# Two graph-attention layers on one core: layer 2's score rows made between the layers and kept in SBUF, its rows normalised on VectorE

## The chip, the cores and the metric

The kernel runs on 1 core of one Trainium2 chip. The metric is the device time of one execution in microseconds (us). Before the change it is 506.02 us, the median of 3 runs (504.74 to 507.35).

## What is computed

Two graph-attention layers over 4096 nodes with 64 features each. Each has a residual sum and a layer norm behind it. Cut to what matters:

```python
def _L0_gnn_ref(h, adj, a):                     # layer 1
    e = (h @ a[:D, 0])[:, None] + (h @ a[D:, 0])[None, :]
    e = jnp.where(e > 0, e, 0.01 * e)
    e = jnp.where(adj > 0, e, NEG_INF)
    return jax.nn.softmax(e, axis=1) @ h

def _L1_gnn_ref(x, edge_index, weight_w, weight_a, bias):   # layer 2
    wh = x @ weight_w
    e = (wh @ weight_a[:OUT_C, 0])[:, None] + (wh @ weight_a[OUT_C:, 0])[None, :]
    e = jax.nn.leaky_relu(e, negative_slope=0.01)
    scores = jnp.where(edge_index > 0, e, NEG_INF)
    return jax.nn.softmax(scores, axis=1) @ wh + bias

x = _layernorm(x + _L0_gnn_ref(x, adj, L0_gnn_a), axis=-1)
x = _layernorm(x + _L1_gnn_ref(x, adj, L1_gnn_weight_w, L1_gnn_weight_a, L1_gnn_bias), axis=-1)
```

`adj` is 4096x4096 int32 of zeros and ones, some four ones in a row.

## The kernel before, in words

The exponent of `leaky_relu(s_i + d_j)` is one of two products, `exp(s_i) exp(d_j)` or its power 0.01, by the sign of `s_i + d_j`. So the kernel never makes the 4096x4096 table of exponentials. It makes, in fp8 bytes that hold 0 or 1, a mask of the positive pairs and one of the negative pairs, and multiplies each with a table of the features, scaled by column and split into three bf16 parts.

The 4096 rows are cut into eight blocks of 512 (`NS`), the columns of a block into four granules of 1024 (`NG`, index `g`). For each granule:

- ScalarE makes the signs (`signs`, eight instructions of 128x512, L557): the input is the block's score row, the sum's row part for 512 rows spread over all 128 partitions, the bias is the column part `dcol`. A score row is one matmul of TensorE (`score_row`, L320) into one of two PSUM halves `srow`.
- VectorE ands the signs with the adjacency bytes (`mask`, L820, L823; granules 0 and 1 lie in SBUF in `kept`, granules 2 and 3 are reloaded by SyncE into `turned`).
- TensorE multiplies (`granule`, L418): 64 matmuls of 195 columns into four banks of the PSUM tensor `acc`.

`neg` and `pos` are rings of four granules; ScalarE may start a granule when TensorE is through with the one four before (semaphore `products`). After a block, VectorE reads `acc` (`read_acc`, L829), forms average, residual and moments (`average`, `residual_sum`, `moments`, L847 to L870), GpSimd takes the power -0.5 of the variance (L968) and multiplies the negated mean with it (L972), and ScalarE normalises the four row groups (`normalize`, L570). In layer 1 the result goes to `xn`; in layer 2 to `x1s`, from which SyncE stores.

Each engine runs its own stream, written out by hand. Between the layers TensorE's stream is, in this order: the last granule of layer 1; the turn of block 6's rows (`turn_x1`, L431); the score row of block 1; small products with the source vector (`scores1`, L371); the projection of block 6 (`project`, L401); more `scores1`; turn and projection of block 7; the first part of the column mean (`mean1`, L351); turn and spreading of the column maximum (L334, L338); the rest of `mean1`; the first granule of layer 2. ScalarE copies turned rows and projections (L577, L579, L585) in between, and makes the exponentials (L535, L536). In the loop of layer 2 each pass of TensorE is

```python
            with pe.Fori(1, NS - 2) as s:
                granule(1, s, NG - 1)
                score_row(1, s + 2)
                for g in range(NG - 1):
                    granule(1, s + 1, g)
```

`xy_old` holds layer 1's tables; layer 2's lie in `stage`. The program's functions that the change touches follow.

Of the kernel before, what the change touches and what calls it, by code (L numbers as in the profile page):

```python
# [36 lines left out]
BYTES = 4  # L37
# [5 lines left out]
def gat_kernel(nc, x, adj, a0, w1, a1, bias1, ident, out):  # L43
# [33 lines left out]
    with ctx:  # L77
# [63 lines left out]

        acc = ctx.enter_context(nc.psum_tensor("acc", [P, RB, 512], F32))
# [35 lines left out]
        srow_ready = sem("srow_ready")  # L178
        narrowed = sem("narrowed")
# [116 lines left out]
        def _(pe):  # L296
# [22 lines left out]
            def score_row(layer, s):  # L319
                nc.tensor.matmul(srow[:, bass.ds((s % 2) * 512, 512)], arep[:, layer, :], xT_at(s),  # L320
                                 start=True, stop=True).then_inc(srow_ready, 1)

# [151 lines left out]
            scores1(NS // 2, NS - 2)  # L474
            turn_x1(NS - 1)
# [4 lines left out]
            spread_max(1)  # L480
            mean1(2, NS - 2)

# [19 lines left out]
        def _(act):  # L502
# [40 lines left out]
            def signs(layer, s, g, tiles=range(GT)):  # L543
                k = (layer * NS + s) * NG + g
                if g == 0:
# [8 lines left out]
                o = neg[:, g, :].bitcast(I8).rearrange("p (b i e) -> p b e i", b=GB, e=BYTES)  # L554
                for t in tiles:
                    col = g * GT + t
                    last = nc.scalar.activation(o[:, t // BYTES, t % BYTES, :], srow[:, bass.ds((s % 2) * 512, 512)],  # L557
                                                ACT.Sign, bias=dcol[:, layer, col:col + 1])
# [3 lines left out]
            def normalize(layer, s):  # L562
                k = layer * NS + s
                act.wait_ge(std_ready, 2 * k + 2)
                if layer == 1:
                    act.wait_ge(stored, 16 * (s + 1))
                act.sem_inc(act_turn, 1)
                for r in range(RB):
                    to = x1s[:, r, :] if layer else xn[:, row_at(s, r), :].rearrange("p o d -> p (o d)")
                    last = nc.scalar.activation(to, y[:, r, :], ACT.Identity, bias=shift_n[:, r:r + 1],  # L570
                                                scale=rstd[:, r:r + 1])
# [443 lines left out]
```

## Time and profile before

| what | value |
|---|---|
| median of 3 runs | 506.02 us |
| profiled execution, its own time | 507.45 us |
| its span, first to last instruction | 505.7 us |
| busy share TensorE / VectorE / ScalarE / GpSimd | 88% / 80% / 79% / 18% |
| mean granted clock of TensorE over the span | 0.926 of full speed |
| HBM read, written | 77.74 MB, 9.44 MB |

The span is that of one execution of the program taken by the hardware profiler. Layer 1 lasts until some 285 us of it and streams the adjacency from HBM; layer 2 works on bytes that are on the chip or reloaded. A row of a view names the engine, the line of the program, what is written and read, and times in us. PE is TensorE, ACT is ScalarE, DVE is VectorE, POOL is GpSimd. PEclk is the granted clock of TensorE as a share of 2.4 GHz. A float32 matmul shows as two records. The share of a whole span is an average over stages with different limits, so the text goes by stretches.

### The profile page before, as it was taken

Reading aid. Unit: us, or ns where it says so; the run is one execution under the profiler, and the core shown is the slowest. Engines: PE = TensorE matmul, PEld = TensorE weight load, DVE = VectorE, ACT = ScalarE, POOL = GpSimd, SP = SyncE. Lnnn points to the kernel's source line nnn. Section 1 sums busy time; section 2 is a strip of 40 time slices with the busy share of each in tenths; the row PEclk is TensorE's granted clock in tenths of the full one; section 3 lists DMA queues with packets and bytes.
Section 4 is the critical chain, followed back from the end, with each engine's and each line's share of the span. In section 5 each row is a group of like instructions: output and inputs, shape, how many; then the busy total and the mean of one; then the engine's idle time right before and its main releaser. Section 6 shows DMA issues by size and latency. Waiting matters only on the chain.

```text
span 505.7 us, 11789 instructions
## 1 busy us (share of the span) xinstructions
PE 447.5 (88%) x4420; PEld 417.1 (82%) x4420; DVE 402.2 (80%) x712; ACT 397.8 (79%) x619; POOL 90.4 (18%) x68
## 2 busy tenths in 40 slices
PE   0799778879979899897979979999999999999991
PEld 0379768868979698797969968999999999999991
DVE  3789989889799898989887889794849586675844
ACT  2695269877978879887890938899899999999931
POOL 0012221514225151421423020010101010101010
PEclk9987979997979999897997958999999999999997
DMA  8999999999999999999973100202030202102000
GB/s 186 251 237 277 286 262 291 313 303 312 313 312 329 302 324 315 319 306 318 329 207 126 43 0 3 84 2 96 1 93 0 93 10 83 55 38 93 3 12 10
DMA packets 80294, 87.71 MB, mean 173 GB/s; under 512 B 7298, under 2 KB 76162, under 8 KB 80258
## 3 DMA queue, kind: packets, MB, share of 16 engines
q1 hardware_dynamic: 45602, 52.98, 36.9%
q10 hardware_dynamic: 34656, 34.21, 25.0%
q8 instruction: 27, 0.44, 0.4%
q14 instruction: 9, 0.07, 0.0%
HBM read 77.74 MB, written 9.44 MB: 172 GB/s over the span
## 4 chain that ended last, share of the span: by engine, by line
issue 49%; DVE 22%; DMA 18%; PE 5%; POOL 4%; SPq 1%; ACT 0%; POOLq 0%; ACTq 0%; DVEq 0%
DMA stage<-in_adj 16%; DVE narrow L791 4%; PE acc L418 4%; DVE turned L803 3%; POOL small L968 3%; DVE pos L817 2%; DMA xn<-in_x 2%; DVE num L854 1%; DVE num L861 1%; DVE red L847 1%; DVE kept L728 1%; DVE bn L866 1%; DVE num L851 1%; DVE kept L725 1%; DVE neg L820 1%
## 5 line engine op out<-in xcount | busy, mean ns | idle before, releaser
L557 ACT ACTIVATE neg<-srow,dcol 128x512 int8 (+1 forms) x512 | 352.9, 880 | 10.4 <-issue 8.0
L418 PE MATMUL acc<-xy_old,pos 128*128 128x195 bf16 x1024 | 198.9, 263 | 22.8 <-POOL pos L979 20.0
L418 PE MATMUL acc<-xy_old,neg 128*128 128x195 bf16 x1024 | 198.6, 263 | 0.0
L418 PE MATMUL acc<-stage,pos 128*128 128x195 bf16 x1024 | 178.2, 248 | 0.0
L418 PE MATMUL acc<-stage,neg 128*128 128x195 bf16 x1024 | 178.1, 248 | 0.0
L418 PEld LDWEIGHTS acc<-xy_old,pos 128*128 128x128 fp8e4 x1024 | 107.5, 105 | 31.7 <-issue 29.8
L418 PEld LDWEIGHTS acc<-xy_old,neg 128*128 128x128 fp8e4 x1024 | 106.8, 104 | 1.6
L418 PEld LDWEIGHTS acc<-stage,pos 128*128 128x128 fp8e4 x1024 | 100.8, 98 | 4.7 <-issue 4.5
L418 PEld LDWEIGHTS acc<-stage,neg 128*128 128x128 fp8e4 x1024 | 100.3, 98 | 0.3 <-issue 0.3
L791 DVE TENSOR_SCALAR narrow<-stage 128x4096 uint8<-128x4096 int32 x32 | 74.1, 2316 | 16.3 <-DMA stage<-in_adj 15.4
L968 POOL TENSOR_TENSOR small<-small,minus_half 128x4 f32<-128x4 f32 x16 | 36.6, 2288 | 210.7 <-DVE small L869 210.7
L820 DVE TENSOR_TENSOR neg<-neg,kept 128x1024 uint32<-128x1024 uint32 x32 | 39.1, 1223 | 31.5 <-ACT neg L557 30.9
L829 DVE TENSOR_REDUCE red<-acc 128x130 f32<-128x390 f32 x64 | 33.1, 553 | 21.3 <-PE acc L418 21.2
L979 POOL TENSOR_TENSOR pos<-kept,neg 128x512 uint32<-128x512 uint32 x16 | 22.3, 1392 | 142.5 <-DVE neg L820 142.5
L820 DVE TENSOR_TENSOR neg<-neg,turned 128x1024 uint32<-128x1024 uint32 x32 | 39.2, 1224 | 2.2 <-ACT neg L557 1.7
L979 POOL TENSOR_TENSOR pos<-turned,neg 128x512 uint32<-128x512 uint32 x16 | 22.3, 1393 | 54.6 <-DVE neg L820 53.8
L570 ACT ACTIVATE x1s<-num,small 128x64 f32<-128x64 f32 x32 | 11.5, 429 | 20.9 <-POOL small L972 20.7
L570 ACT ACTIVATE xn<-num,small 128x64 f32 (+1 forms) x32 | 11.5, 429 | 18.9 <-POOL small L972 18.9
L315 PE MATMUL acc<-idf,xn 128*64 128x128 f32 x32 | 7.2, 418 | 15.8 <-DMA xn<-in_x 15.8
L315 PEld LDWEIGHTS acc<-idf,xn 128*64 128x64 f32 x32 | 5.2, 170 | 18.4 <-issue 12.2
L823 DVE TENSOR_TENSOR pos<-turned,neg 128x1024 uint32<-128x1024 uint32 x16 | 19.6, 1224 | 0.6
L823 DVE TENSOR_TENSOR pos<-kept,neg 128x1024 uint32<-128x1024 uint32 x16 | 19.6, 1224 | 0.5
(117 smaller groups left out, 337.2 us busy)
## 6 DMA issues: line engine op xcount, KB each, us to landing
stage<-in_adj ACTq DMA_DIRECT2D x64, 512.0 KB, 9.2
stage<-in_adj SPq DMA_DIRECT2D x64, 512.0 KB, 9.4
spill<-turned SPq DMA_DIRECT2D x16, 512.0 KB, 7.5
turned<-spill SPq DMA_DIRECT2D x16, 512.0 KB, 3.8
out<-x1s SPq DMA_DIRECT2D x8, 128.0 KB, 1.9
xn<-in_x SPq DMA_DIRECT2D x1, 768.0 KB, 17.0
kept<-in_x SPq DMA_DIRECT2D x4, 128.0 KB, 3.9
kept<-in_x ACTq DMA_DIRECT2D x4, 128.0 KB, 5.0
```

The costliest lines, as they stand in the source:

```text
L315: last = nc.tensor.transpose(acc[0:D, t % RB, b * P:(b + 1) * P], xn[:, t // 2 * (2 * RB) + t % 2 + 2 * b, :], idf[:, :])
L418: last = nc.tensor.matmul(acc[:, r, c * XW:(c + 1) * XW], masks[c][:, t // BYTES, t % BYTES, r * P:(r + 1) * P], xy[layer][:, g * GT + t, ...
L557: last = nc.scalar.activation(o[:, t // BYTES, t % BYTES, :], srow[:, bass.ds((s % 2) * 512, 512)], ACT.Sign, bias=dcol[:, layer, col:col ...
L570: last = nc.scalar.activation(to, y[:, r, :], ACT.Identity, bias=shift_n[:, r:r + 1], scale=rstd[:, r:r + 1])
L791: nc.vector.tensor_scalar(narrow[:, 0:GN].rearrange("p (b g j) -> p g b j", b=GB, g=GR), stage[:, g % SLOTS, :].rearrange("p (g b j) -> p ...
L803: nc.vector.transpose(words(mask_at(s, g)), words(narrow[:, 0:GN])).then_inc(turned_ready, 1)
L817: nc.vector.scalar_tensor_tensor(words(pos[:, g, :])[:, half], c[:, half], CODES, a[:, half], ALU.bitwise_xor, ALU.bitwise_and).then_inc(p ...
L820: nc.vector.tensor_tensor(c, c, a, ALU.bitwise_and).then_inc(neg_ready, 1)
L823: nc.vector.tensor_tensor(words(pos[:, g, :]), a, c, ALU.bitwise_xor).then_inc(pos_ready, 1)
L829: nc.vector.tensor_reduce(red[:, r, :, :].rearrange("p c f -> p (c f)").rearrange("p (c f) -> p c f", c=2), acc[:, r, 0:2 * XW].rearrange( ...
L968: nc.gpsimd.tensor_tensor(rstd, var, minus_half[:, :], ALU.pow).then_inc(std_ready, 1)
L979: nc.gpsimd.tensor_tensor(pos[:, g, :].bitcast(U32)[:, half], mask_at(s, g).bitcast(U32)[:, half], neg[:, g, :].bitcast(U32)[:, half], ALU ...
```

## The change

It has two parts.

The score rows of blocks 2 to 7 of layer 2 are no longer made in layer 2's loop. TensorE makes rows 2 to 5 ahead of the turn of block 7, into the four banks of `acc`, and rows 6 and 7 behind the spreading of the column maximum (`score_rows`). ScalarE copies them in two instructions (`keep_rows`) into `rows_sb`, which lies over `xy_old`; layer 2's signs read them there from block 2 on. Blocks 0 and 1 read `srow` as before.

Layer 2's normalising leaves ScalarE. VectorE does it in four instructions (`normalize1`) behind the mask of the next block's granule 2, with the mean and GpSimd's power; GpSimd's second product and VectorE's negated mean fall away in layer 2.

```diff
+        rows_sb = xy_old[:, :].bitcast(F32)[:, 0:(NS - 2) * SUP].rearrange("p (s n) -> p s n", n=SUP)
...
+            def score_rows(first, end):
+
+                for s in range(first, end):
+                    last = nc.tensor.matmul(acc[:, (s - 2) % RB, :], arep[:, 1, :], xT_at(s), start=True, stop=True)
+                last.then_inc(rows_psum, 1)
...
             scores1(NS // 2, NS - 2)
+            pe.wait_ge(acc_read, NS * RB + RB)
+            score_rows(2, NS - 2)
             turn_x1(NS - 1)
...
             spread_max(1)
+            pe.wait_ge(rows_kept, 1)
+            score_rows(NS - 2, NS)
             mean1(2, NS - 2)
+            pe.wait_ge(rows_kept, 2)
 
             granule(1, 0, 0)
...
-            score_row(1, 2)
-            for g in range(NG - 1):
-                granule(1, 1, g)
-            with pe.Fori(1, NS - 2) as s:
-                granule(1, s, NG - 1)
-                score_row(1, s + 2)
-                for g in range(NG - 1):
-                    granule(1, s + 1, g)
-            granule(1, NS - 2, NG - 1)
-            for g in range(NG):
-                granule(1, NS - 1, g)
+            with pe.Fori(1, NS) as s:
+                for g in range(NG):
+                    granule(1, s, g)
...
+            def keep_rows(first, end):
+                n = end - first
+                act.wait_ge(rows_psum, 1 if first == 2 else 2)
+                act.wait_ge(products, FREE_AT_FIRST + NS * NG * RB)
+                nc.scalar.copy(rows_sb[:, first - 2:end - 2, :], acc[:, 0:n, :]).then_inc(rows_kept, 1)
...
             copy_wh(NS - 2)
-            normalize(0, NS - 1)
+            keep_rows(2, NS - 2)
+            normalize(NS - 1)
             copy_x1(NS - 1)
             copy_wh(NS - 1)
             act.wait_ge(shift_ready, 4)
             exps(1, slice(NEAR, TILES), minus_shift[:, 1, 0:1], minus_shift[:, 1, 1:2], far_exp)
+            keep_rows(NS - 2, NS)
             for g in range(2, NG):
                 signs(1, 0, g)
             signs(1, 1, 0)
             row_factors(1)
-            with act.Fori(0, NS - 2) as s:
-                for g in range(1, NG):
-                    signs(1, s + 1, g)
-                normalize(1, s)
-                signs(1, s + 2, 0)
             for g in range(1, NG):
-                signs(1, NS - 1, g)
-            normalize(1, NS - 2)
-            normalize(1, NS - 1)
+                signs(1, 1, g)
+            act.wait_ge(rows_kept, 2)
+            with act.Fori(2, NS) as s:
+                for g in range(NG):
+                    signs(1, s, g)
...
+            def normalize1(s):
+
+                dve.wait_ge(stored, 16 * (s + 1))
+                dve.wait_ge(std_ready, 2 * NS + s + 1)
+                dve.sem_inc(dve_turn, 1)
+                for r in blocks:
+                    last = V.tensor_scalar(x1s[:, r, :], y[:, r, :], mv[:, r, 0:1], rstd[:, r:r + 1],
+                                           ALU.subtract, ALU.mult)
+                last.then_inc(x1_ready, 1)
```

TensorE between the layers, from the second group of small products to the first granule of layer 2. Before:

```order
L371 MATMUL misc<-v_src,xT 128x1 x8
L431 MATMUL flip<-idf,xn 64x128 x4
L401 MATMUL misc<-wext,xTs 128x65 x4
L351 MATMUL flip<-wh,onesN 128x256 x2
L334 MATMUL misc<-idf,mcol 1x128
L338 MATMUL misc<-mcol,one_row 128x1
L351 MATMUL flip<-wh,onesN 128x256 x4
L418 MATMUL acc<-stage,pos 128x195
```

With the change (its lines have moved by up to 10):

```order
L381 MATMUL misc<-v_src,xT 128x1 x8
L330 MATMUL acc<-xT,arep 128x512 x4
L441 MATMUL flip<-idf,xn 64x128 x4
L411 MATMUL misc<-wext,xTs 128x65 x4
L361 MATMUL flip<-wh,onesN 128x256 x2
L344 MATMUL misc<-idf,mcol 1x128
L348 MATMUL misc<-mcol,one_row 128x1
L330 MATMUL acc<-xT,arep 128x512 x2
L361 MATMUL flip<-wh,onesN 128x256 x4
L428 MATMUL acc<-stage,pos 128x195
```

Two groups of score rows have come in (L330), one ahead of the turn of block 7's rows, one ahead of the rest of the column mean.

ScalarE in the same place, from the copy of block 6's projection to the signs of layer 2's first block. Before:

```order
L585 COPY wh<-misc 128x4x65
L570 ACTIVATE xn<-num,small 128x64 x4
L577 COPY xTs<-flip 64x4x2x32x2
L579 COPY xT<-flip 64x512
L585 COPY wh<-misc 128x4x65
L535 ACTIVATE wts<-dcol,minus_shift 128x16
L536 ACTIVATE wts<-dcol,minus_shift 128x16
L557 ACTIVATE neg<-srow,dcol 128x512 x24
```

With the change:

```order
L598 COPY wh<-misc 128x4x65
L592 COPY xy_old<-acc 128x2048
L577 ACTIVATE xn<-num,small 128x64 x4
L584 COPY xTs<-flip 64x4x2x32x2
L586 COPY xT<-flip 64x512
L598 COPY wh<-misc 128x4x65
L542 ACTIVATE wts<-dcol,minus_shift 128x16
L543 ACTIVATE wts<-dcol,minus_shift 128x16
L592 COPY xy_old<-acc 128x1024
L569 ACTIVATE neg<-srow,dcol 128x512 x24
```

The copy of four score rows stands ahead of the normalising of block 7, the copy of two ahead of the signs.

VectorE in the loop of layer 2, from the moments to the loop's end (ISA and REGISTER_ALU are address work). Before:

```order
L868 BN_AGGR mv<-bn 128x2 x4
L837 REGISTER_ALU
L869 TENSOR_SCALAR small<-mv 128x4
L870 TENSOR_SCALAR small<-mv 128x4
L810 REGISTER_ALU
L814 ISA
L820 TENSOR_TENSOR neg<-neg,turned 128x1024
L823 TENSOR_TENSOR pos<-turned,neg 128x1024
L944 REGISTER_ALU
```

With the change:

```order
L880 BN_AGGR mv<-bn 128x2 x4
L849 REGISTER_ALU
L881 TENSOR_SCALAR small<-mv 128x4
L822 REGISTER_ALU
L826 ISA
L832 TENSOR_TENSOR neg<-neg,turned 128x1024
L835 TENSOR_TENSOR pos<-turned,neg 128x1024
L888 REGISTER_ALU
L891 TENSOR_SCALAR x1s<-num,mv,small 128x64 x4
L968 REGISTER_ALU
```

The negated mean (L870) is gone, and the four normalising instructions (L891) stand behind the mask of granule 2.

## Rows read from the trace of the kernel before

**Rows 1.** By stretch: busy PE, PEld, DVE, ACT, POOL (instructions), PEclk, DMA share, GB/s.

```profile
390.00:413.30 23.30, 23.30 (x261) 22.38 (x259) 16.20 (x35) 23.26 (x37) 2.29 (x2) 1.00 0.15 51
262.00:265.00 3.00, 0.03 (x1) 0.00 (x0) 2.86 (x4) 3.00 (x5) 1.25 (x1) 0.79 0.02 6
265.10:270.60 5.50, 5.49 (x34) 5.05 (x35) 5.40 (x10) 1.01 (x3) 0.48 (x1) 0.50 0.25 100
291.10:308.10 17.00, 13.96 (x51) 11.22 (x51) 14.93 (x30) 7.16 (x15) 3.00 (x2) 0.50 0.00 1
```

**Rows 2.** Timeline of ScalarE and GpSimd in layer 2: start, length, instructions.

```profile
390.10 1.44 ACT L570 ACTIVATE x1s<-num,small 128x64 f32<-128x64 f32 x4
391.44 21.92 ACT L557 ACTIVATE neg<-srow,dcol 128x512 int8 x32
413.40 1.44 ACT L570 ACTIVATE x1s<-num,small 128x64 f32<-128x64 f32 x4
...
460.00 1.44 ACT L570 ACTIVATE x1s<-num,small 128x64 f32<-128x64 f32 x4
...
483.25 1.10 ACT L570 ACTIVATE x1s<-num,small 128x64 f32<-128x64 f32 x3
387.41 2.05 POOL L968 TENSOR_TENSOR small<-small,minus_half 128x4 f32<-128x4 f32 x1 [20.80 <-DVE small L869]
389.66 0.25 POOL L972 TENSOR_TENSOR small<-small 128x4 f32<-128x4 f32 x1 [0.20 <-POOL small L968]
```

**Rows 3.** Timeline of ScalarE between the layers.

```profile
294.94 1.44 ACT L570 ACTIVATE xn<-num,small 128x64 f32<-128x64 f32 x4 [2.85 <-POOL small L972]
...
323.16 0.26 ACT L541 ACTIVATE ab<-ab 128x64 f32<-128x64 f32 x1 [1.14 <-DVE ab L715]
```

**Rows 4.** Timeline of TensorE between the layers.

```profile
292.14 3.57 PE L371 MATMUL misc<-v_src,xT 64*128 64x1 f32 x16 [0.55 <-ACT wh L585]
296.52 1.03 PE L431 MATMUL flip<-idf,xn 128*64 128x128 f32 x4 [0.81 <-ACT xn L570]
298.87 1.94 PE L401 MATMUL misc<-wext,xTs 65*128 65x65 f32 x8 [1.32 <-ACT xTs L577]
...
303.20 0.58 PE L338 MATMUL misc<-mcol,one_row 1*128 1x1 f32 x2 [0.37 <-DVE mcol L745]
303.71 3.78 PE L351 MATMUL flip<-wh,onesN 128*128 128x256 f32 x8
307.29 0.37 PE L418 MATMUL acc<-stage,pos 128*128 128x195 bf16 x1
```

**Rows 5.** Timeline of TensorE around a score row in layer 2.

```profile
379.22 0.25 PE L418 MATMUL acc<-stage,neg 128*128 128x195 bf16 x1
379.39 1.12 PE L320 MATMUL srow<-xT,arep 64*128 x2
380.45 0.26 PE L418 MATMUL acc<-stage,pos 128*128 128x195 bf16 x1
```

**Rows 6.** Timeline of VectorE in the same block: the residual sum, the mask.

```profile
385.07 0.87 DVE L861 SCALAR_TENSOR_TENSOR num<-num,small,xn 128x64 f32<-128x64 f32 x4
...
387.36 1.23 DVE L820 TENSOR_TENSOR neg<-neg,turned 128x1024 uint32<-128x1024 uint32 x1
```

**Rows 7.** Timeline of TensorE: eight records of 512 columns at the full clock.

```profile
27.50 3.97 PE L345 MATMUL flip<-xn,onesN 128*128 128x512 f32 x8
```

**Rows 8.** ScalarE's copies by form: busy time, mean ns of one.

```profile
L528 ACT COPY xT<-acc 64x512 f32<-64x512 f32 x8 | 4.6, 579 | 4.2 <-PE acc L315 4.2
L516 ACT COPY kept<-kept 128x2048 f32<-128x2048 f32 x1 | 1.9, 1899 | 2.6 <-DMA kept<-in_x 2.6
...
L585 ACT COPY wh<-misc 128x260 f32<-128x260 f32 x3 | 1.2, 395 | 1.9 <-PE misc L401 1.8
```

**Rows 9.** Timeline of GpSimd and ScalarE at the end.

```profile
500.37 1.01 POOL L968 TENSOR_TENSOR small<-small,minus_half 128x4 f32<-128x4 f32 x1 [17.26 <-DVE small L869]
501.92 1.43 ACT L570 ACTIVATE x1s<-num,small 128x64 f32<-128x64 f32 x4 [17.24 <-POOL small L972]
```

More of the change, by code:

```diff
@@ L178, in gat_kernel @@
         srow_ready = sem("srow_ready")
+        rows_psum = sem("rows_psum")
+        rows_kept = sem("rows_kept")
         narrowed = sem("narrowed")
@@ L544, in signs @@
                 k = (layer * NS + s) * NG + g
-                if g == 0:
+                kept_row = layer == 1 and not (isinstance(s, int) and s < 2)
+                if g == 0 and not kept_row:
                     act.wait_ge(srow_ready, layer * NS + s + 1)
@@ L554, in signs, with normalize @@
                 o = neg[:, g, :].bitcast(I8).rearrange("p (b i e) -> p b e i", b=GB, e=BYTES)
+                if kept_row:
+                    row = rows_sb[:, bass.ds(s - 2, 1), :].rearrange("p o n -> p (o n)")
+                else:
+                    row = srow[:, bass.ds((s % 2) * 512, 512)]
                 for t in tiles:
                     col = g * GT + t
-                    last = nc.scalar.activation(o[:, t // BYTES, t % BYTES, :], srow[:, bass.ds((s % 2) * 512, 512)],
-                                                ACT.Sign, bias=dcol[:, layer, col:col + 1])
+                    last = nc.scalar.activation(o[:, t // BYTES, t % BYTES, :], row, ACT.Sign, bias=dcol[:, layer, col:col + 1])
                 if tiles[-1] == GT - 1:
                     last.then_inc(signs_ready, 1)
[L562 to L566, printed above, removed]
+            def normalize(s):
+                act.wait_ge(std_ready, 2 * s + 2)
                 act.sem_inc(act_turn, 1)
                 for r in range(RB):
-                    to = x1s[:, r, :] if layer else xn[:, row_at(s, r), :].rearrange("p o d -> p (o d)")
-                    last = nc.scalar.activation(to, y[:, r, :], ACT.Identity, bias=shift_n[:, r:r + 1],
-                                                scale=rstd[:, r:r + 1])
+                    last = nc.scalar.activation(xn[:, row_at(s, r), :].rearrange("p o d -> p (o d)"), y[:, r, :],
+                                                ACT.Identity, bias=shift_n[:, r:r + 1], scale=rstd[:, r:r + 1])
                 last.then_inc(x1_ready, 1)
@@ L599, in body0 @@
                     copy_wh(s - 1)
-                normalize(0, s)
+                normalize(s)
             tables0()
@@ L619, in _ @@
             copy_wh(NS - 3)
-            normalize(0, NS - 2)
+            normalize(NS - 2)
             act.wait_ge(shift_ready, 3)
@@ L869, in moments @@
                 V.tensor_scalar(var, mv[:, :, 1], EPS, None, ALU.add).then_inc(var_ready, 1)
-                V.tensor_scalar(minus_mean, mv[:, :, 0], -1.0, None, ALU.mult).then_inc(mean_turned, 1)
+                if layer == 0:
+                    V.tensor_scalar(minus_mean, mv[:, :, 0], -1.0, None, ALU.mult).then_inc(mean_turned, 1)
+            def normalize1(s):
[6 more added lines that the diff above has]
+                last.then_inc(x1_ready, 1)
             def body0(s):
@@ L943, in _ @@
             mask(1, 1, 2)
+            normalize1(0)
             with dve.Fori(1, NS - 1) as s:
@@ L954, in _ @@
                         moments(1, s)
+                normalize1(s)
             mask(1, NS - 1, NG - 1)
@@ L959, in _ @@
             moments(1, NS - 1)
+            normalize1(NS - 1)
         @block.gpsimd
@@ L964, in inverse_std @@
             def inverse_std(layer, s):
-                k = layer * NS + s
-                pool.wait_ge(var_ready, k + 1)
+                pool.wait_ge(var_ready, layer * NS + s + 1)
+                pool.sem_inc(pool_turn, 1)
                 nc.gpsimd.tensor_tensor(rstd, var, minus_half[:, :], ALU.pow).then_inc(std_ready, 1)
-                pool.wait_ge(std_ready, 2 * k + 1)
-                pool.wait_ge(mean_turned, k + 1)
+                if layer == 1:
+                    return
+                pool.wait_ge(std_ready, 2 * s + 1)
+                pool.wait_ge(mean_turned, s + 1)
                 pool.sem_inc(pool_turn, 1)
```

## The prediction

> **What bounds the kernel now.** I read the busy time by stretch first. In one period of layer 2, 390.0 to 413.3 us, TensorE is busy for 23.30 of 23.30 us and ScalarE for 23.26, VectorE for 16.20 and GpSimd for 2.29 [rows 1]. Two engines look full, and one of them must be waiting. ScalarE's timeline tells which [rows 2]: its four normalising instructions start at 390.10 and 413.40 us, 23.30 us apart, and 390.10 is 0.19 us after GpSimd's second product has ended (389.66 plus 0.25). GpSimd follows VectorE, and VectorE the block's last product, so ScalarE is tied to TensorE's pace. The last block, in which TensorE makes no score row, shows ScalarE's own pace: 460.00 to 483.25 is 23.25 us. TensorE bounds layer 2, and ScalarE has next to nothing to spare.
>
> Between the layers it is different. From 291.1 to 308.1 us TensorE is granted half its clock (0.50, the 1.2 GHz level, [rows 1]) and waits for a chain [rows 3, 4]: normalise the last rows of layer 1 (ScalarE, 294.94), turn them (TensorE, 296.52), copy (ScalarE), project (TensorE, 298.87), copy (ScalarE), the maximum over the columns (TensorE, until 303.20), the rest of the column mean (303.71), and only then the first granule of layer 2 (307.29). From there TensorE streams to the last block. What delays this chain delays the end, and what leaves TensorE's stream in layer 2 brings the end forward, one to one.
>
> **The change part by part.**
>
> *Score rows leave the loop.* The block's last record starts at 379.22, the row's two records at 379.39, the next block's first at 380.45 [rows 5]. Of these 1.23 us one record of the granules would take 0.09 (256 of them fill the rest of the 23.30), so a row costs 1.14 us. Six of them (blocks 2 to 7) leave TensorE's full stream: 6 x 1.14 = **-6.9 us**, and the period becomes 22.15 us.
>
> *Normalising leaves ScalarE.* Its 1.34 us per block (390.10 to 391.44, [rows 2]) buy nothing by themselves, since TensorE bounds. They are needed as room: 32 sign instructions take 21.92 us, just under the new 22.15. VectorE takes the step over. Four of its instructions of 128x64 with two tensors to read take 0.87 us [rows 6]; the new ones read one, so 0.87 is the upper bound and I take 0.8. VectorE's 16.20 us of a period become 17.0 of 22.15. The new wait for GpSimd's power (387.41 plus 2.05, [rows 2]) stands behind the mask of granule 2, two instructions of 1.23 us from 387.36 to 389.84 [rows 6], so it has ended by then: nothing. Queued behind the wait is the mask of granule 3: 389.84 plus 0.8 plus about 2.5 is 393.1, and TensorE, which is through with the block before at 379.4 [rows 5], wants it three granules (5.54 us each, a quarter of 22.15) later, at 396.0: nothing. Tighter is the mask of granule 2: it is done at 389.84, and without the score row TensorE wants it two granules after 379.4, at 390.5. It holds by 0.6 us: nothing. The wait for the last store is a wait for a transfer issued a block earlier. SyncE stores when the normalising is done, which moves from 391.5 (390.10 plus 1.44) to 390.6: the reloads queued behind it aren't late.
>
> *Four score rows ahead of the last turn.* They stand behind the sixteen small products of 292.14, which are through at about 295.6, and ahead of the turn of 296.52 [rows 4]. ScalarE's copy of them stands ahead of the normalising that starts at 294.94 [rows 3]. So both engines hold the chain. Price: in layer 1's column mean four full-width products (eight records) took 3.97 us at the full clock [rows 7], 3.5 without the tail that overlaps the next. At half clock eight half-width records take 3.78 us (303.71, [rows 4]), 0.43 each; at full width 0.85 to 0.87, 7.0 us for eight. The copy of 128x2048 follows; ScalarE's one copy of that size took 1.90 us [rows 8]. The normalising starts at 303.9 in place of 294.94: **+9.0 us**. Bounds: all at the full clock 299.3, +6.2; no rise 302.8, +9.7.
>
> *Two more rows ahead of the rest of the mean.* TensorE idles between the steps of the delayed chain, as in the 1.32 us before 298.87, so I expect half clock again: +3.6 us for two rows (1.9 at full). They start TensorE's stream about 4 us ahead of the mean, so the clock comes back within it and saves 1.1 of its 3.6 us, and the first granule runs at the full clock, 0.4 us less: **+2.1 us**; bounds -0.3 (all at full) and +3.6. ScalarE's copy of the two (half of 1.90) runs beside the mean. It pushes the signs behind it by 1 us against the chain; ScalarE idles 1.14 us before 323.16, at their end [rows 3], and the first of them are for a granule that TensorE begins two granules, 11 us, after the first: nothing.
>
> *The tail.* Now: power to 501.38, the second product, ScalarE from 501.92 for 1.43 us [rows 9], 503.35. Then: power to 501.38, 0.1 of signalling, 0.8 on VectorE, 502.3: **-1.05 us**.
>
> Sum: -6.9 + 9.0 + 2.1 - 1.05 = **+3.15 us**, on the profiled execution's 507.45 us (span 505.7). That execution stands 1.4 us above the median of the three runs, 506.02, within their spread; against the median I forecast **509.2 us**, 0.6% slower. What counts as a difference is 0.5% (2.5 us), about what a measurement can tell from no change.
>
> **A cost I put at nothing.** The source of the signs moves from PSUM to SBUF. ScalarE's copies out of PSUM take 0.38 to 0.40 us for 260 elements and 0.58 for 512, so 0.19 us for 252 elements; carried on to 2048 elements that is 1.74, and the SBUF copy took 1.90 [rows 8]. An instruction that reads SBUF may take up to 0.16 us longer. But a sign lasts 0.88 us and one starts every 0.685, so 0.2 us of each is overlapped. Between 0 and 0.16 I take 0, since a fixed latency is what overlaps. The Trainium skill, "Advanced Engine Details and Errata", section The Read-Write Bubble, says that memory latency shows between ScalarE's instructions and that this engine is closer to PSUM; by it the signs would come further apart, and the second rival would be the outcome.
>
> **The rivals.**
>
> *The clock holds (faster).* The moved rows keep or bring back 2.4 GHz at once, and it stays through the chain: +6.2 in place of +9.0. The turn and the projection, 1.03 and 1.94 us at half clock [rows 4], take half: -1.5. The second place gives -0.3. Sum: -6.9 + 6.2 - 1.5 - 0.3 - 1.05 = -3.55, **502.5 us**. For it: the added work is dense. Against it: the copy and the normalising leave TensorE idle for over 3 us right behind the rows, and after it had idled from 262 to 265 us it was granted 0.50 until 270.6 [rows 1]. Chance 0.12.
>
> *ScalarE becomes the bound (slower still).* This decides from 22.15/32 = 0.692 us per sign on; now it is 0.685. With half of the 0.16 us, 0.765, a period is 24.5 us, 2.3 above the new one: 6 x 2.3 = 14 us; with 0.05, 23.5 us, 8 us. Of this ScalarE can work off some 4 us ahead, in a ring of four granules. So 4 to 10 us over my sum, **513 to 519 us**. For it: the margin is 0.2 us a block. Against it: no row shows a source in SBUF that starts less often. By the skill's rule above this one would be the likelier. Chance 0.12.
>
> *The clock returns sooner (no change).* A rise 2 to 3 us sooner at either place takes 1 to 1.5 us off the sum, at both 2 to 3: 506.2 to 508.2, within 0.5%. Two rises are few to time it by (5.5 and 4.9 us), and the three runs differ by 2.6 us as it is. Chance 0.33.
>
> *The mask of granule 2 is late.* Each 0.6 us beyond its margin adds 0.6 x 7 = 4 us, 513. Chance 0.03.
>
> **How the numbers follow.** My forecast has 0.40. Slower by over 0.5%: 0.40 + 0.12 + 0.03 = 0.55; within 0.5%: 0.33; faster: 0.12. The range leaves out the faster rival and the worse part of the ScalarE one: **504.0 to 513.5 us**.
>
> **What would show it.** Right: TensorE's period in layer 2 at 22.15 us, without gaps; four products of 512 columns starting near 295.6 and taking over 6 us, mostly at half clock; the last normalising of layer 1 near 304; the first granule of layer 2 near 319 in place of 307.3; ScalarE waiting for products in layer 2. Wrong: a granted clock of 1.0 through the rows and the chain; the first granule before 315; signs every 0.69 us or more, with VectorE waiting for ScalarE and TensorE for masks; TensorE waiting for the mask of granule 2 alone.

## The result and the profile after

The changed kernel takes 512.54 us (median of 4 runs, 511.97 to 512.73), the kernel before 505.38 us (4 runs, 504.41 to 507.35): ratio 1.0125, 95% interval 1.0098 to 1.0151. It is slower, as forecast (509.2 us), and by about twice the amount. A second measurement, the last run below, gives 512.49 against 506.41 us and the same ratio.

The stretches of layer 2 first, in the view of [rows 1] (us, busy PE, PEld, DVE, ACT, POOL with their instructions, granted clock, DMA share, GB/s):

```profile
397.20:419.30 22.10, 22.10 (x258) 22.10 (x256) 17.01 (x39) 22.10 (x33) 1.95 (x1) 1.00 0.18 53
262.00:288.40 26.40, 22.99 (x242) 21.92 (x240) 23.43 (x53) 18.11 (x32) 5.75 (x5) 1.00 0.26 88
288.50:319.10 30.60, 25.01 (x66) 15.65 (x66) 17.66 (x38) 9.85 (x17) 2.90 (x2) 0.50 0.00 0
302.60:305.80 3.20, 0.00 (x0) 0.00 (x0) 0.00 (x0) 3.13 (x5) 0.00 (x0) 0.50 0.00 0
```

TensorE is full in layer 2 as before. Between the layers it is at half clock for 30.7 us in place of 17.1, and for 3.2 us in the middle it does nothing while ScalarE copies and normalises. GpSimd's powers give the length of a block in layer 2:

```profile
397.24 1.95 POOL L994 TENSOR_TENSOR small<-small,minus_half 128x4 f32<-128x4 f32 x1 [20.20 <-DVE small L881]
419.39 1.94 POOL L994 TENSOR_TENSOR small<-small,minus_half 128x4 f32<-128x4 f32 x1 [20.20 <-DVE small L881]
```

That is 22.15 us, against 23.30 before [rows 2]. TensorE between the layers, to be laid beside [rows 4]:

```profile
289.37 1.97 PE L411 MATMUL misc<-wext,xTs 65*128 65x65 f32 x8
291.89 3.57 PE L381 MATMUL misc<-v_src,xT 64*128 64x1 f32 x16 [0.55 <-ACT wh L598]
295.32 7.17 PE L330 MATMUL acc<-xT,arep 64*128 64x512 f32 x8
305.87 1.03 PE L441 MATMUL flip<-idf,xn 128*64 128x128 f32 x4 [3.38 <-ACT xn L577]
308.20 1.94 PE L411 MATMUL misc<-wext,xTs 65*128 65x65 f32 x8 [1.29 <-ACT xTs L584]
...
312.54 0.58 PE L348 MATMUL misc<-mcol,one_row 1*128 1x1 f32 x2 [0.37 <-DVE mcol L757]
313.05 3.78 PE L330 MATMUL acc<-xT,arep 64*128 64x512 f32 x4
316.76 3.17 PE L361 MATMUL flip<-wh,onesN 128*128 128x256 f32 x8
319.76 0.25 PE L428 MATMUL acc<-stage,pos 128*128 128x195 bf16 x1
```

and ScalarE, beside [rows 3]:

```profile
302.53 1.87 ACT L592 COPY xy_old<-acc 128x2048 f32<-128x2048 f32 x1 [10.70 <-PE acc L330]
304.29 1.43 ACT L577 ACTIVATE xn<-num,small 128x64 f32<-128x64 f32 x4
...
316.86 1.01 ACT L592 COPY xy_old<-acc 128x1024 f32<-128x1024 f32 x1 [1.93 <-PE acc L330]
```

The eight records of the four rows take 7.17 us, ScalarE has waited 10.70 us for them, then come its copy and the normalising, then the turn: the chain that the prediction named. At the end, beside [rows 9]:

```profile
505.56 1.01 POOL L994 TENSOR_TENSOR small<-small,minus_half 128x4 f32<-128x4 f32 x1 [17.82 <-DVE small L881]
506.70 0.98 DVE L891 TENSOR_SCALAR x1s<-num,mv,small 128x64 f32<-128x64 f32 x4 [1.32 <-POOL small L994]
```

Layer 1 ends at another moment in each execution. The clock there falls and rises at moments that differ (in the profile of before it is at half from 263.8 to 270.6, in that of the changed kernel not at all between 262 and 288.4), so the two profiles are compared from the start of layer 1's last product, which is 285.16 us before and 283.82 after:

```profile
283.82 0.25 PE L428 MATMUL acc<-xy_old,neg 128*128 128x195 bf16 x1
```

All following "from layer 1's end" are differences of such starts in one trace, in us:

| kernel | last normalising of layer 1 | first granule of layer 2 | first to last product of layer 2 | from there to the end | whole |
|---|---|---|---|---|---|
| before | 9.77 | 22.13 | 187.27 | 11.11 | 220.50 |
| before again | 9.77 | 22.13 | 187.24 | 11.12 | 220.48 |
| changed | 20.47 | 35.94 | 179.89 | 10.39 | 226.22 |

The change costs 13.8 us up to the first granule, gives back 7.4 in layer 2 and 0.7 at the end: 5.7 us more. In layer 2 ScalarE makes its signs without a pause, so it is not the one that waits there; TensorE isn't kept waiting either.

### The profile page after: what moved, and what is told of

The parts are those of the page before. It is cut to its first block, busy times and chain, and to the rows that moved or that the text cites. A ratio compares the mean times of both kernels' runs of the same rounds, so it can differ in the third digit from the quotient of the medians.

```text
span 510.0 us, 11757 instructions
## 1 busy us (share of the span) xinstructions
PE 448.0 (88%) x4420; PEld 417.5 (82%) x4420; DVE 409.5 (80%) x736; ACT 395.3 (77%) x589; POOL 86.9 (17%) x60
## 4 chain that ended last, share of the span: by engine, by line
PE 44%; DVE 22%; DMA 20%; issue 11%; SPq 1%; ACT 1%; ACTq 0%; POOL 0%; DVEq 0%; POOLq 0%
PE acc L428 37%; DMA stage<-in_adj 19%; DVE narrow L803 5%; DVE turned L815 4%; DVE pos L829 2%; PE acc L330 2%; PE misc L381 1%; DVE num L873 1%; DMA kept<-in_x 1%; PE flip L361 1%; DVE num L866 1%; DVE red L859 1%; PE misc L411 1%; DVE kept L740 1%; DVE bn L878 1%
## 5 line engine op out<-in xcount | busy, mean ns | idle before, releaser
L569 ACT ACTIVATE neg<-srow,dcol 128x512 int8<-128x512 f32 (+1 forms) x320 | 222.0, 855 | 12.8 <-issue 9.6
L428 PE MATMUL acc<-xy_old,pos 128*128 128x195 bf16 x1024 | 195.1, 260 | 22.9 <-POOL pos L1007 19.3
L428 PE MATMUL acc<-xy_old,neg 128*128 128x195 bf16 x1024 | 194.9, 261 | 0.0
L569 ACT ACTIVATE neg<-xy_old,dcol 128x512 int8 x192 | 137.3, 874 | 0.0
L428 PEld LDWEIGHTS acc<-xy_old,pos 128*128 128x128 fp8e4 x1024 | 106.2, 104 | 31.2 <-issue 29.9
L428 PEld LDWEIGHTS acc<-xy_old,neg 128*128 128x128 fp8e4 x1024 | 105.7, 103 | 1.3
L994 POOL TENSOR_TENSOR small<-small,minus_half 128x4 f32<-128x4 f32 x16 | 35.1, 2193 | 219.7 <-DVE small L881 219.7
L577 ACT ACTIVATE xn<-num,small 128x64 f32 (+1 forms) x32 | 11.5, 430 | 13.0 <-POOL small L1000 12.7
L411 PE MATMUL misc<-wext,xTs 65*128 65x65 f32 x64 | 11.5, 339 | 9.6 <-ACT xTs L584 9.6
L815 DVE STREAM_TRANSPOSE kept<-narrow 128x1024 uint32<-128x1024 uint32 x16 | 19.8, 1238 | 0.1
```

What stands on the lines that cost most here:

```text
L411: last = nc.tensor.matmul(wh_psum[:, e * E:(e + 1) * E], cols[:, e], wext1[:, :], start=True, stop=True)
L428: last = nc.tensor.matmul(acc[:, r, c * XW:(c + 1) * XW], masks[c][:, t // BYTES, t % BYTES, r * P:(r + 1) * P], xy[layer][:, g * GT + t, ...
L577: last = nc.scalar.activation(xn[:, row_at(s, r), :].rearrange("p o d -> p (o d)"), y[:, r, :], ACT.Identity, bias=shift_n[:, r:r + 1], sc ...
L815: nc.vector.transpose(words(mask_at(s, g)), words(narrow[:, 0:GN])).then_inc(turned_ready, 1)
L994: nc.gpsimd.tensor_tensor(rstd, var, minus_half[:, :], ALU.pow).then_inc(std_ready, 1)
```

## The experiments

Theory: the four rows and their copy stand in the one chain that decides when layer 2 starts; the gain in the loop is real but smaller; nothing else of the change costs anything. Rivals: the normalising on VectorE or the signs' source in SBUF costs time in layer 2; TensorE's added time counts wherever it stands; the difference comes from the executions of before.

**The kernel before, again.** No edit.

> The kernel before, unchanged, to see what its executions differ in: the change came out 4.5 us longer between the two profiled executions and 7.2 us between the medians. Theory A: the granted clock between the layers comes and goes at other moments in other executions of before, so this profile, if it is of a shorter execution (505 us or less), shows a stretch at half clock that is shorter than the 17.1 us (291.1 to 308.1) of the first one. Theory B: layer 1 ends at another moment (the loads from HBM), and the stretch between the layers takes the same: then the moments of layer 1's block 7, at 291.5 us before, come 2 us sooner and all behind them with them.

506.53 us (10 runs, 504.87 to 509.89), ratio 1.0006 (0.9978 to 1.0035) against before measured beside it. In its profile, of an execution of 508.35 us, layer 1's last product starts at 286.08 us, 0.9 later than in the first one. From there the two agree to 0.02 us (table), and the stretch at half clock is again 17.1 us long:

```profile
291.90:309.00 17.10, 14.11 (x52) 11.38 (x52) 15.03 (x30) 7.24 (x15) 3.00 (x2) 0.50 0.01 1
```

So for this kernel it is theory B: what varies lies ahead of the end of layer 1. (Theory A was tied to a shorter execution and this one is longer, but its half-clock stretch didn't move at all.) In the changed kernel the stretch itself varies too, as the last run shows. The difference of two profiles' totals (4.5 us here) says less than the stretch from layer 1's end (5.7 us).

**Only the normalising moved.** The kernel before with this part of the change; score rows stay in the loop. The main lines:

```diff
-                normalize(1, s)              # ScalarE's loop of layer 2, and the two behind it
+                normalize1(s)                # VectorE's loop, as in the change
...
```

> Only layer 2's normalising goes to VectorE; score rows stay in the loop. Theory: TensorE bounds layer 2 at 23.30 us a block with or without it, so only the end gains: one us less, 504.4 us against 505.4. Rival (VectorE's wait for GpSimd costs time in each block): the block takes longer than 23.30 us and the kernel is slower than before by some multiple of 7.

505.54 us, ratio 0.9982 (0.9957 to 1.0008): no difference that can be told in the total. Its trace shows the expected: blocks of 23.3 us, by GpSimd's powers

```profile
385.79 1.94 POOL L980 TENSOR_TENSOR small<-small,minus_half 128x4 f32<-128x4 f32 x1 [21.37 <-DVE small L866]
409.08 1.94 POOL L980 TENSOR_TENSOR small<-small,minus_half 128x4 f32<-128x4 f32 x1 [21.36 <-DVE small L866]
```

and 22.11 us from layer 1's end to the first granule, and 10.34 in place of 11.11 us at the end, 219.6 in all. VectorE loses nothing by its wait, so this part of the change is worth 0.8 to 0.9 us and costs nothing.

**Only the rows moved.** The changed kernel with layer 2's normalising back on ScalarE; the lines of ScalarE's stream:

```diff
             act.wait_ge(rows_kept, 2)
-            with act.Fori(2, NS) as s:
-                for g in range(NG):
-                    signs(1, s, g)
+            normalize(0, 1)
+            signs(1, 2, 0)
+            with act.Fori(1, NS - 2) as s:
+                for g in range(1, NG):
+                    signs(1, s + 1, g)
+                normalize(s, 1)
+                signs(1, s + 2, 0)
...
```

> Only the score rows are moved; ScalarE still normalises layer 2. Theory: the first granule of layer 2 comes as late as in the changed kernel (some 12.5 us later than before), and in layer 2 ScalarE, which needs 23.25 us a block by its own pace (last block of before), bounds in TensorE's place, so almost nothing of the 6.9 us comes back: 505.4 + 12 = 517 to 518 us, block 23.2 us. Rival (ScalarE works ahead in its ring or its own pace is shorter than that): blocks of 22.2 us and 513.5 us, which is the changed kernel plus the 1 us of the tail.

521.67 us, ratio 1.0302 (1.0256 to 1.0348), more than either side expected. The first granule comes at 35.95 us from layer 1's end, as in the changed kernel. The blocks are longer than before, 24.17 us:

```profile
403.30 22.97 ACT L569 ACTIVATE neg<-xy_old,dcol 128x512 int8 x32
426.14 1.41 ACT L581 ACTIVATE x1s<-num,small 128x64 f32<-128x64 f32 x4
427.45 23.01 ACT L569 ACTIVATE neg<-xy_old,dcol 128x512 int8 x32
450.34 1.08 ACT L581 ACTIVATE x1s<-num,small 128x64 f32<-128x64 f32 x3
```

ScalarE bounds, as the theory says, but 32 signs take 23.0 us where they took 21.92 [rows 2]. They read SBUF now. In the traces a sign that reads PSUM starts 0.674 us behind the one before it, one that reads SBUF 0.715 us, in every kernel with both. TensorE and VectorE wait for it (a window of one block, in the view of groups; behind the bar busy time and mean ns, then the idle time before, and what ended it):

```profile
L428 PE MATMUL acc<-stage,pos 128*128 128x195 bf16 x120 | 21.0, 247 | 1.7 <-DVE pos L847 1.4 <-DVE red L853 0.3
...
L844 DVE TENSOR_TENSOR neg<-neg,kept 128x1024 uint32<-128x1024 uint32 x2 | 2.5, 1225 | 5.9 <-ACT neg L569 5.9
```

So the cost that the prediction put at nothing is there, 0.041 us a sign. In the changed kernel it is hidden behind TensorE: its 192 signs from SBUF take 137.3 us, 22.9 us a block against TensorE's 22.15.

```profile
L569 ACT ACTIVATE neg<-xy_old,dcol 128x512 int8 x192 | 137.3, 874 | 0.0
```

Over six blocks ScalarE falls 4.4 us behind TensorE, and it had the lead for it. The signs of a block's first granule end 10.3 us ahead of TensorE's start on it in block 2, and 6.75 us ahead in block 7, where that granule's masks are still 4.1 us early. In the kernel of this run TensorE waits for masks when the signs are 3.0 to 4.4 us ahead. The lead shrinks by 0.7 us a block and is 6.2 us at the last granule, so by an estimate from these numbers three or four more blocks would make ScalarE the bound. Moving the normalising is what makes room: with it on ScalarE the same rows cost 9 us more.

**The four rows behind the turn.**

```diff
-            score_rows(2, NS - 2)
             turn_x1(NS - 1)
+            score_rows(2, NS - 2)
...
-            keep_rows(2, NS - 2)
             normalize(NS - 1)
             copy_x1(NS - 1)
+            keep_rows(2, NS - 2)
```

> The changed kernel with the four rows behind the turn of block 7 in place of ahead of it, and ScalarE's copy of them behind the normalising and the copies of the turned rows. Same instructions, other order. Theory: the rows (7 us at half clock) then delay only the projection; ScalarE's copy of 1.9 us runs beside it and the idle 0.9 us ahead of the turn and 1.3 us behind it are used: block 7's projection is copied at about 305 us in place of 310.3, 5 us less, 507.4 us. Rival (what counts is TensorE's added time between the layers, wherever it stands): 512.5 us as before.

509.21 us, ratio 1.0052 (1.0028 to 1.0076): 3.3 us less than the changed kernel, not 5. From layer 1's end the last normalising is back at 9.74 us, the copy of block 7's projection starts at 21.4 in place of 26.4 us, the forecast 5.0 less, the first granule at 31.5 in place of 35.9, and to the end it is 222.6 us, 3.6 less. The missing part is the clock: here layer 2's first granule starts 1.7 us before it rises and takes 6.3 us in place of 5.5, and the mean ahead of it runs wholly at half clock, 0.6 us longer than in the changed kernel. The place of the rows counts, and the rival is out.

```profile
295.87 1.03 PE L441 MATMUL flip<-idf,xn 128*64 128x128 f32 x4 [0.73 <-issue]
296.83 7.19 PE L330 MATMUL acc<-xT,arep 64*128 64x512 f32 x8
303.96 1.97 PE L411 MATMUL misc<-wext,xTs 65*128 65x65 f32 x8
...
312.54 3.78 PE L361 MATMUL flip<-wh,onesN 128*128 128x256 f32 x8
316.12 0.37 PE L428 MATMUL acc<-stage,pos 128*128 128x195 bf16 x1
```

**Rows 128 partitions deep.** The rows of blocks 2 to 7 are made of other operands and aren't score rows.

```diff
-                    last = nc.tensor.matmul(acc[:, (s - 2) % RB, :], arep[:, 1, :], xT_at(s), start=True, stop=True)
+                    last = nc.tensor.matmul(acc[:, (s - 2) % RB, :], onesN[:, :],
+                                            xn[:, 0:8, :].rearrange("p b d -> p (b d)"), start=True, stop=True)
```

> The changed kernel, but the six moved score rows are products of two other float32 operands that fill all 128 partitions instead of 64 (a table of ones over 4096 with eight row blocks), so the rows of blocks 2 to 7 hold other numbers than the score rows; number of products, columns and passes are the same. In the changed kernel the clock stayed at 1.2 GHz through 7.0 us of dense rows (64 partitions deep) and rose after the mean's 128-deep products. Theory (rows that use half the array's depth don't bring the clock back): now it rises inside the first rows, 3 to 6 us after they start, and the last of the eight records ends 0.5 to 2 us sooner; the same at the second place: 509 to 511.5 us against 512.5. Rival (float32 products as such, or just chance, left the clock low): half clock from 288 to 319 as before, 512.5 us.

509.20 us (10 runs, 508.34 to 513.42), ratio 1.0068 (1.0044 to 1.0091), 3.3 us less than the changed kernel. The profile is of its longest execution (513.42, layer 1 ends at 287.26 us), so I read the stretch, first TensorE's row in the timeline, then three stretches in the view of [rows 1]:

```profile
297.64 6.61 PE L330 MATMUL acc<-xn,onesN 128*128 128x512 f32 x8
```

```profile
293.30:303.40 10.10, 9.55 (x25) 6.11 (x25) 9.83 (x13) 0.74 (x2) 2.90 (x2) 0.50 0.00 0
303.50:306.80 3.30, 0.74 (x2) 0.00 (x0) 0.25 (x1) 2.52 (x4) 0.00 (x0) 1.00 0.00 0
307.00:320.50 13.50, 11.21 (x28) 7.25 (x29) 5.95 (x17) 4.70 (x10) 0.00 (x0) 0.50 0.00 1
```

The clock rose 5.9 us after the rows had started, for 3.4 us, and fell again in the idle time behind them. The rows took 6.61 us in place of 7.17. In the four profiles with float32 rows 64 deep (7.0 us of them or more on end) it never rose there. At the second place the rise came 5.8 us after the start of the two rows here, and 6.1 to 9.2 us after it in the five profiles with float32 rows 64 deep.

From layer 1's end it is 224.2 us, 2.0 less than in the changed kernel, but 1.1 of this is not the rows: they start 10.4 us behind that end in place of 11.5, since the clock fell later (6.0 us behind it, not 4.6). The shorter rows are 0.6 us and the second place 0.3. Where the rest of the 3.3 us between the medians comes from, one profile doesn't show.

Number, columns and type of the products are the same in both kernels; what differs are the operands, 64 or 128 deep and with other values. The runs don't part depth from values; depth is what I take for the cause, and it is not shown.

**Keeping the clock up.** On top of the kernel with only the normalising moved (a wait for free banks of `acc` and one more group of three are left out here):

```diff
+            def keep_warm(n):
+                for _ in range(n):
+                    nc.tensor.matmul(acc[:, RB - 1, 0:256], onesN[:, :].bitcast(BF16)[:, 0:P],
+                                     onesN[:, :].bitcast(BF16), start=True, stop=True)
...
+            scores1(0, NS // 2, 1)            # one behind each small product
             project(NS - 2)
+            keep_warm(8)
...
+            scores1(NS // 2, NS - 2, 1)
+            keep_warm(6)
             turn_x1(NS - 1)
+            keep_warm(10)
```

> The kernel with only the normalising moved (505.5 us), with extra products between the layers whose result nobody reads: one bf16 product of 256 columns, 128 deep, behind each of the 24 small products, and groups of 8, 6, 10 and 3 where TensorE waits for block 6's copy, block 7's rows, their copy, and the column maximum. They fill about 5 us of TensorE's idle time at the full clock. Theory: from the last layer-1 product to the first layer-2 granule it is 22.1 us, of which TensorE's share at half clock would be some 4 us less at the full one; if the clock holds, this stretch falls to 18 to 19 us and the kernel to 502 us. Rival (the many one-column products keep the clock from holding): the clock falls all the same, the extra products then take twice as long and delay the turn of block 7 by 2 to 5 us: 507 to 510 us.

515.95 us, ratio 1.0191 (1.0160 to 1.0222): the rival, and worse than it said.

```profile
284.80:290.70 5.90, 5.90 (x35) 3.95 (x32) 5.51 (x23) 5.90 (x10) 0.00 (x0) 1.00 0.00 0
290.80:311.20 20.40, 20.40 (x83) 15.09 (x84) 10.17 (x13) 3.51 (x8) 2.90 (x2) 0.50 0.00 1
```

TensorE is busy all the time and still falls to half clock at 290.8, after a stream that is mostly small products. At half clock a filler takes 0.21 us within a group, and 0.39 us behind a small product (a pair takes 0.84 us, a small product alone 0.45), and the turn of block 7 starts at 308.25 us, 12 later than in before.

**The four rows in one pass.** They are made of the upper halves of both float32 factors (bf16), so rounded.

```diff
+            def upper(ap):
+                return ap.bitcast(BF16).rearrange("p (n h) -> p n h", h=2)[:, :, 1]
...
+                    a, b = (arep[:, 1, :], xT_at(s)) if first > 2 else (upper(arep[:, 1, :]), upper(xT_at(s)))
...
```

> The changed kernel, but the four score rows ahead of the turn are made of the upper halves (bf16) of both factors, in one pass instead of four, so they are rounded. Theory: at half clock they take 4 x 0.43 = 1.7 us in place of 7.0, ScalarE's copy ahead of the normalising stays: the last normalising of layer 1 starts 5.3 us sooner, and so does all behind it: 507.2 us. What is left of the delay there, against before, is then the copy and 1.7 us less the 0.9 idle. Rival (the copy and the order, not the products, hold the chain): less than 3 us gained.

507.79 us, ratio 1.0040 (1.0013 to 1.0068), 4.7 us less than the changed kernel. Its last normalising comes at 14.70 us from layer 1's end in place of 20.47, 5.8 less:

```profile
294.67 1.86 PE L335 MATMUL acc<-xT,arep 64*128 64x512 bf16 x4
296.57 1.86 ACT L597 COPY xy_old<-acc 128x2048 f32<-128x2048 f32 x1 [5.39 <-PE acc L335]
298.33 1.44 ACT L582 ACTIVATE xn<-num,small 128x64 f32<-128x64 f32 x4
```

The four rows take 1.86 us in place of 7.17, about a quarter, which fits one pass in place of four. So of the 10.7 us by which the changed kernel delays this step, 5.8 are the three further passes (5.3 of it) and a later start, and the other 4.9 stay: one pass, the copy, and the small products that end behind the moment at which the normalising could start. To the end it is 221.9 us, 4.4 less than in the changed kernel, since here the clock comes back 1.8 us after layer 2 has begun.

**One-pass rows in the loop.** The kernel with only the normalising moved, all layer 2 rows rounded as above, made in the loop.

```diff
             def score_row(layer, s):
-                nc.tensor.matmul(srow[:, bass.ds((s % 2) * 512, 512)], arep[:, layer, :], xT_at(s),
+                a, b = (upper(arep[:, 1, :]), upper(xT_at(s))) if layer else (arep[:, 0, :], xT_at(s))
+                nc.tensor.matmul(srow[:, bass.ds((s % 2) * 512, 512)], a, b,
...
```

> The kernel with only the normalising moved, score rows in the loop as before, but all of layer 2's score rows made of the upper halves (bf16) of both factors, in one pass, so they are rounded. Theory: TensorE bounds layer 2, a row costs it 0.3 us or so in place of 1.14, the block takes 22.4 to 22.5 us in place of 23.30, and nothing is added between the layers: six blocks give 5 us, 500.5 us. Rival (ScalarE, at 32 signs of 0.673 us = 21.5 us a block, or VectorE's mask of granule 2, with under 1 us to spare, takes over): blocks of over 22.7 us and 502 us or more.

501.69 us, ratio 0.9914 (0.9881 to 0.9948). The block takes 22.57 us, so a row costs 0.42 in place of 1.14 us (22.15 without), a little more than the 0.3 expected; neither ScalarE nor the mask takes over. From layer 1's end it is 215.1 us, 5.4 less than before, with 22.11 us to the first granule.

```profile
400.41 0.25 PE L423 MATMUL acc<-stage,neg 128*128 128x195 bf16 x1
400.59 0.40 PE L325 MATMUL srow<-xT,arep 64*128 x1
400.91 0.26 PE L423 MATMUL acc<-stage,pos 128*128 128x195 bf16 x1
```

**Cheap rows, moved, behind the turn.** The changed kernel with both edits: `upper` for all six rows, and the order of the run with the rows behind the turn.

> The changed kernel with all six moved rows made in one pass of the upper halves (bf16) of both factors, so rounded, and the first four behind the turn of block 7, their copy behind the copies of the turned rows. Theory: at half clock four rows take 1.7 us, of which TensorE has 1.3 to 1.5 us idle behind the turn, two more take 0.9 us, and the loop keeps its 22.15 us a block: from the last layer-1 product to the first layer-2 granule 23 to 23.5 us in place of 22.1, to the end 214.2 us (before 220.5, one-pass rows in the loop 215.1): 501 us. Rival (signs that read SBUF, 0.714 us each and so 22.9 us a block, have less work in hand ahead here, since layer 2 starts sooner, and TensorE waits for masks): blocks of over 22.3 us towards the end, 503 us or more.

499.72 us, ratio 0.9860 (0.9835 to 0.9886): the shortest median, and faster than both kernels. Against the cheap rows in the loop (0.9881 to 0.9948) the intervals touch, and from layer 1's end the two profiles differ by 0.35 us only, so whether the move pays beside the cheap rows is not settled.

```profile
296.32 1.03 PE L446 MATMUL flip<-idf,xn 128*64 128x128 f32 x4
297.29 1.88 PE L335 MATMUL acc<-xT,arep 64*128 64x512 bf16 x4
299.10 1.97 PE L416 MATMUL misc<-wext,xTs 65*128 65x65 f32 x8
...
303.98 1.03 PE L335 MATMUL acc<-xT,arep 64*128 64x512 bf16 x2
```

Behind the turn TensorE now makes the four rows in the time in which it would wait for the copy of the turned rows. From layer 1's end it is 23.5 us to the first granule (22.1 before) and 214.75 to the end (215.10 with the cheap rows in the loop); blocks of 22.14 us to the last. Signs from SBUF have 6.7 us in hand in the last block, so this rival didn't come.

**The changed kernel, again.** No edit.

> The changed kernel, unchanged, for more executions beside those of before, whose times ranged from 504.2 to 508.7 us while the four of the changed one lay between 512.0 and 512.7. Theory (layer 1 ends sooner or later by up to 2.5 us with the moments at which the clock is halved there, in either kernel; what the change does is the 5.7 us between the last layer-1 product and the end): over more executions the changed kernel spreads over 510 to 514 us as well, and the ratio comes down to 1.010 to 1.012. Rival (the changed kernel is steadier, and before's median of four is its true one): the same 512.5 us and 1.0125 or more.

512.49 us (6 runs, 511.05 to 513.93) against 506.41 (10 runs), ratio 1.0125 (1.0098 to 1.0152). It does spread more widely, by 2.9 us, while the ratio stays: half of the theory. Its profile has 227.9 us from layer 1's end, with 34.1 us at half clock in place of 30.7, so where the clock falls and rises is worth 1.6 us between two executions of this kernel.

## Why the prediction was right, and where it was off

By its own terms, sum and measured stretch (changed less before, from layer 1's end):

| term | forecast | measured |
|---|---|---|
| four rows and copy ahead of the turn | +9.0 | +10.7 (20.47 less 9.77) |
| two rows ahead of the mean, with the first granule | +2.1 | +2.7 (13.81 less 10.70, less 0.40 for the granule) |
| six rows out of the loop | -6.9 | -7.0 (7.38 less the same 0.40) |
| the tail | -1.05 | -0.7 |
| sum | +3.15 | +5.7 |

The main mechanism was right: TensorE bounds layer 2, a row costs it 1.14 us there (blocks of 22.15 us), VectorE hides the normalising, the mask of granule 2 holds by 0.5 us (the prediction had 0.6), and the chain between the layers pays for the rows. One of its own signs of being right didn't come: ScalarE doesn't wait for products in layer 2. Part of a sign of being wrong did: signs out of SBUF start every 0.715 us, but TensorE never waits for masks.

That the total lies inside the range, 1 us below its end, is luck. With both chain terms at their own upper bounds the sum is -6.9 + 9.7 + 3.6 - 1.05 = +5.35 us, 511.4 us. The measured 512.54 us, and the 5.7 us of the stretch, lie above that. The range reached to 513.5 us for a part of the ScalarE rival, and that one didn't happen.

What was mis-sized most is the first term, by 1.7 us, in two parts (0.7 and 1.1, and a copy 0.1 shorter).

*The clock.* The step "I take the rise after 5.5 us, with 6.3 of eight records done" failed. The rise was timed by stretches in which TensorE had mostly made products 128 partitions deep; score rows are 64 deep, and through 7.17 us of them the clock stayed at half. The run with 128-deep rows of other values showed a rise after 5.9 us. This is 0.7 us here, within the term's own upper bound (no rise, +9.7). At the second place the clock came back within the mean, as forecast, but later, at 319.2 us: the mean took 3.17 us in place of 3.78, so 0.6 us was saved and not 1.1, and the two rows cost 3.7 and not 3.6.

*The start.* "Through at about 295.6" was taken from before, 10.4 us behind layer 1's end. In the changed kernel's execution the clock fell 4.6 us behind that end, and not 5.9, so the small products took 4.04 us in place of 3.63 and the projection 1.97 in place of 1.30, and the rows started at 295.32, 11.5 us behind it: 1.1 us. The moment of the fall doesn't come from the change: in the ten profiles whose streams are the same up to there (all but the one with fillers and that with cheap rows in the loop) it lies 4.4 to 6.0 us behind layer 1's end. In before it is hidden, since TensorE waits 0.81 us for the normalising ahead of the turn anyway; with rows in front of the turn it counts.

*The tail* gave 0.3 us less. Four instructions on VectorE took 0.98 us and not 0.8, above the bound of 0.87 that came from others of the same size; that is 0.2 of it.

*The base.* The prediction went from 506.02 us, the median of three. The measured medians differ by 6.1 to 7.2 us where the stretch behind layer 1 differs by 5.7 (7.4 with the second profile of the changed kernel). What is between them can be layer 1's end, which differs by 0.8 to 0.9 us between two profiles of the same kernel, or this stretch, which differs by 1.6 us in the changed one; the two profiles of each don't tell.

*The rivals.* The clock did not hold, and it returned later at both places, not sooner. The masks of granule 2 were not late. ScalarE's rival had its price right and its outcome wrong. The price is 0.041 us a sign, inside the stated 0 to 0.16 and beyond the deciding point (0.715 against 0.692 us a sign). The prediction's 0.685 was 21.92 us over 32 signs, which counts the last one's tail; start to start it is 0.674. Its 0.16 came from copies of up to 512 elements carried on to 2048; the changed kernel's copy of that size out of PSUM took 1.87 us, against 1.90 from SBUF. And it took 0 "since a fixed latency is what overlaps": that was wrong, this latency doesn't overlap.

The rule from the Trainium skill, "Advanced Engine Details and Errata", section The Read-Write Bubble, is that memory latency shows between ScalarE's instructions, and that this engine is closer to PSUM. The traces agree: 0.674 us from start to start out of PSUM, 0.715 out of SBUF.

At that pace ScalarE needs 22.9 us a block. That TensorE's block still was 22.15 is a matter of six blocks and a ring: the lead was 10.3 us in block 2 and not some 4, and 4.0 of it was used up by the last granule (10.3 to 6.2).

## What to carry to other kernels

Work that is taken out of a full engine's loop is free only where that engine is idle and nobody waits for it; ask what chain runs through the gap, at which clock, and what each engine has queued behind the moved piece. Here a row cost 1.14 us in the loop and 1.8 us (7.17 for four) at half clock between the layers, plus a copy, on the path. Making the piece cheap (one pass for a row that only feeds a sign, if the rounding is acceptable) brought the time down where moving it had raised it. With cheap rows the move no longer costs; the 0.35 us by which it is ahead in the profiles is too little to call a gain. Compare two profiles from a common event; here the end of layer 1 lies between 283.1 and 287.3 us in twelve profiles, whose kernels are the same up to there, and the change is worth 5.7 us.

## What the runs showed of the hardware that was not expected

- TensorE stayed at 1.2 GHz through 7.2 us of float32 products of 512 columns on 64 partitions, in four profiles, and rose 5.9 us after the start of products of the same shape on 128 partitions, with other values (one profile).
- It fell to 1.2 GHz while busy without a gap, in a mix of one-column products and single ones of 256 columns (284.8 to 290.7 us at 1.00, then 0.50).
- A sign of 128x512 with bytes as output starts 0.674 us behind the last one from PSUM and 0.715 us from SBUF, back to back; 32 of them take 21.92 and 23.0 us.
- A float32 row of 512 columns in the stream of layer 2 (fp8 weights, 195 bf16 columns) costs 1.14 us at the full clock, in one bf16 pass 0.42 us.
